# Last edge layer of a graph network: relation matrices as two fp16 parts instead of three bf16 parts, and 91 instead of 96 supertiles read from a table

## The chip, the cores and the metric

One Trainium2 chip, one core of it. The metric is the device time of one execution in microseconds (us), lower is better. A core has five engines with queues of their own: PE (TensorE, matrix products), DVE (VectorE), ACT (ScalarE), POOL (GpSimd) and SP (SyncE, which here only starts transfers). They meet through semaphores.

## What is computed

Four graph layers over 6250 nodes with 16 features and 206250 edges sorted by destination. The first runs on a dense adjacency matrix; the second gathers typed rows (8 edge types); the third is dense again; the fourth, which is changed here, is an edge layer with 90 relation types:

```
W_rel = matmul(w_comp, V).reshape(90, 16, 16)
h_src = h[src];  z_src = h_src @ Ws.T;  z_dst = h[dst] @ Ws.T;  z_e = he @ Ws.T
e   = concatenate([z_src, z_e, z_dst]) @ Wa.T
msg = einsum('ei,eio->eo', h_src, W_rel[rel_type]) * e
h_out = segment_sum(msg, dst)
x = x + h_out
```

## The kernel before

Edges are cut into tiles of 128, and eight tiles make a supertile of 1024 edges; there are 202 supertiles. In the last layer (`relation_layer`) each supertile is of one of three kinds, given by the line `PLAIN, LEAD, DIRECT = 11, 2, 96`.

- Plain, the first 11. POOL fetches the source rows h[src] by eight indirect transfers (L2191). Meanwhile PE builds a table in memory, for every node and every relation the finished product of row and matrix (`table_tile`, L2158, 49 tiles with three matmuls each; ACT and DVE evict them, SP stores them).
- Table, 96 of the other 191. POOL fetches the finished products by eight indirect transfers of 128 rows each (`fetch_table_rows`, L2205) into a ring of 12 row buffers. A buffer is free again when PE has summed the supertile that used it. DVE then only compares destinations (`make_dst`, L2230) and scales rows (`weigh_rows`, L2317, L2318).
- Matmul, the remaining 95. DVE writes one-hots of the source (`make_hot`, seven `tensor_scalar` at L2220 and L2221) and of the type (L2225, 90 partitions by 1024 edges). PE gathers the rows with 28 matmuls of 512 columns (`gather`, L2239), folds them with 16 small ones (`fold_rows`, L2254), and expands the type one-hots into one 16 by 16 matrix for each edge (`expand`, L2274).

The plain kind uses `expand` too, so `expand` runs for 106 supertiles. For each of the eight tiles of a supertile it makes three matmuls into the same half of a PSUM bank, one for each part of the relation matrices: `rel[:, 0..2, :]` holds a bf16 value, the bf16 remainder and the remainder of that. So there are 24 matmuls of 256 columns, with the type one-hots as the stationary operand (128 columns, 90 rows). DVE multiplies the result by the gathered rows and reduces it (`messages`, L2302 and L2294), and PE sums messages by destination (`add_up`, L2326).

The main loop runs over the supertiles that are not table ones, in rounds. In round i, PE's order is: fold and expand supertile i-1, gather supertile i, add up supertile i-2, and add up the table supertiles that lie behind i-2. DVE's order is: table rows behind i-2, one-hots of i+1, destinations and messages of i-1. A set of one-hots has two buffers, so DVE's `make_hot(i+1)` waits for PE's gather of i-1 (a semaphore). ACT takes the four gather banks out (L2245), then the folded rows (L2262), then the sums (L2337). POOL does nothing but fetch table rows. Which supertiles are table ones is spread evenly by integer division, about one between any two matmul ones.

The relation matrices are prepared much earlier, at the end of POOL's side work of the first layer (`split_relations`, L1614 to L1619): a load, a transposing copy, and four operations that make the three parts. The first layer has six dense passes (`one_pass`, 0 to 5) in which DVE scales a PSUM bank for each chunk of 448 nodes (L1420) and makes the next table.

Of the kernel before, what the change touches and what calls it, by code (L numbers as in the profile page):

```python
# [7 lines left out]
ALU = mybir.AluOpType  # L8
ACT = mybir.ActivationFunctionType
AX = mybir.AxisListType  # L10

P = 128
# [36 lines left out]
TOP = 14  # L49
# [17 lines left out]
LEAD1, DIRECT1, ROWS_AHEAD = 3, 80, 12  # L67
PLAIN, LEAD, DIRECT = 11, 2, 96
SPLIT_FROM = 4
# [52 lines left out]
def program(nc, t, wcols, out):  # L122
# [15 lines left out]
    def step(eng, ins):  # L138

        return done[eng].by(ins)  # L140

    def link(eng, ins):

        tok = step(eng, ins)
        need(eng, tok)
        return tok

    def sb(stack, name, shape, dt=F32):
        return stack.enter_context(nc.sbuf_tensor(name, list(shape), dt))
# [40 lines left out]
    var = sb(life, "var", [P, NT])  # L190
    rel = sb(life, "rel", [R90, 3, 256], BF16)
    t_u = sb(life, "t_u", [P, 3 * F])
    path = sb(life, "path", [P, 1], I32)
# [1086 lines left out]
    def layers_fast(h_tok):  # L1280
# [279 lines left out]
        def edge_terms(s):  # L1560
# [26 lines left out]
            make_rows(attr, s_attr[0], s_term[0])  # L1587
            split_relations(attr, s_attr[0])
            return [(x.sem, x.n) for x in s_term]

# [20 lines left out]
        def split_relations(attr, s_back):  # L1611

            relO, relT = (a[:, :, :].rearrange("p s c -> p (s c)")[0:R90, 0:256] for a in attr)
            need(pool, s_back.by(pool.dma_start(relO, rel_dram.rearrange("a r c -> (a r c)").rearrange("(r k) -> r k", k=256)), 16))  # L1614
            link(pool, pool.tensor_copy(relT.rearrange("r (o i) -> r o i", i=F), relO.rearrange("r (i o) -> r o i", o=F)))
            link(pool, pool.tensor_copy(rel[:, 0, :], relT))
            link(pool, pool.tensor_tensor(relO, relT, rel[:, 0, :], ALU.subtract))
            link(pool, pool.tensor_copy(rel[:, 1, :], relO))
            link(pool, pool.tensor_tensor(rel[:, 2, :], relO, rel[:, 1, :], ALU.subtract))  # L1619

# [5 lines left out]
        pool.wait_ge(s_used, NCH)  # L1626
        terms = edge_terms(side_work)
        st = one_pass(d, 1, st, [feature(d, "enc1", 128, 128, "enc_b1"), rows_table(d, 0, "enc2", 128, 64)], 64)
        for r in range(4):
# [5 lines left out]
            rows_table(d, 1, "dfc1_w", 32, 64, leaky=True, bias="dfc1_row")], 64)  # L1635
        st = one_pass(d, 3, st, [feature(d, "dec0", 128, 128, "dec_b0"), rows_table(d, 0, "dec1", 128, 64)], 64)
        st = one_pass(d, 4, st, [feature(d, "fold64", 128, 64, "dec_b1"), rows_table(d, 1, "dec2", 64, F)], F)
        d["spread"] = []
# [418 lines left out]
        def relation_layer(x_spread, terms, wx, w_ready):  # L2057
# [150 lines left out]
            def make_hot(i):  # L2208
# [14 lines left out]
                if i >= 3:  # L2223
                    dve.wait_ge(*w_tok[i - 3, SUP // 2 - 1])
                ty_tok[i] = c_ty.by(dve.tensor_scalar(tyh[i % 3][:, :], trow[b][:, :], iotaP[0:R90, :], None, ALU.is_equal))  # L2225

# [37 lines left out]
            def expand(i, between=()):  # L2264
                pe.wait_ge(*ty_tok[i])
                for q in range(SUP // 2):
                    if q == SUP // 4:
                        for m in between:
                            table_tile(m)
                    if i:  # L2270
                        pe.wait_ge(*prod_tok[i - 1, q])
                    for j in (2 * q, 2 * q + 1):
                        for p in range(3):
                            ins = pe.matmul(ps_w[q][:, (j % 2) * 256:(j % 2 + 1) * 256], tyh[i % 3][:, j * P:(j + 1) * P], rel[:, p, :], start=p == 0, stop=p == 2)  # L2274
                    if q % 2:
                        w_tok[i, q - 1] = w_tok[i, q] = c_w.by(ins)
# [260 lines left out]
```

## Time and profile before

| | us |
|---|---|
| median of 3 runs | 4388.06 |
| the three runs | 4388.06, 4360.72, 4389.13 |
| the profiled execution | 4367.42 |
| its span, first to last instruction | 4363.3 |
| PE busy / DVE busy in the span | 3616.4 (83%) / 2704.6 (62%) |
| ACT busy / POOL busy in the span | 1310.6 (30%) / 1907.4 (44%) |

### The profile page before, as it was taken

What the parts mean: (1) busy time and instruction counts of PE and PEld (TensorE: products, weight loads), DVE (VectorE), ACT (ScalarE), POOL (GpSimd) and SP (SyncE); (2) the same over time, 40 slices, a digit from 0 to 9 for tenths busy, and PEclk for the clock granted to TensorE, in tenths of its full rate; (3) what the DMA queues carried; (4) which work ended last, traced back from release to release, by engine and by line L of the source; (5) the groups of instructions that cost most, each with busy time, mean ns of one, the idle gap of its engine ahead of it and who ended that gap; (6) DMA issues with size and microseconds to landing.
All of it is one profiled execution on the core that took longest, in us unless ns stands there. A gap on an engine that the chain in (4) does not pass through costs nothing. (4 is left out here: it accounts for less than half of the span.)

```text
span 4363.3 us, 77744 instructions
## 1 busy us (share of the span) xinstructions
PE 3616.4 (83%) x28548; PEld 2114.8 (48%) x28548; DVE 2704.6 (62%) x6415; ACT 1310.6 (30%) x2874; POOL 1907.4 (44%) x1856
## 2 busy tenths in 40 slices
PE   6787879999998478888888886661899989998888
PEld 4566645544554234444444443330555555555555
DVE  8999953322212356767666674451777767777777
ACT  6999920011000123333233231330222212222222
POOL 1000006830000546777677640357366666666550
PEclk8999989999998689999899897765888888889998
DMA  5444467663366312222222227761222222222221
GB/s 148 83 82 82 66 267 297 218 235 121 151 246 259 88 41 51 51 51 51 47 51 51 51 45 249 271 206 13 41 44 44 44 39 44 44 44 44 39 43 40
DMA packets 471196, 445.62 MB, mean 102 GB/s; under 512 B 357554, under 2 KB 406610, under 8 KB 459676
## 3 DMA queue, kind: packets, MB, share of 16 engines
q1 hardware_dynamic: 389178, 391.82, 29.3%
q0 software_dynamic: 55216, 38.70, 6.4%
q10 hardware_dynamic: 26417, 10.05, 0.9%
q8 instruction: 232, 3.80, 0.4%
q14 instruction: 153, 1.25, 0.1%
HBM read 346.18 MB, written 95.85 MB: 101 GB/s over the span
## 5 line engine op out<-in xcount | busy, mean ns | idle before, releaser
L1814 POOL DMA_INDIRECT rows<-typed_table,ring x640 | 764.1, 1194 | 348.5 <-issue 182.0
L2239 PE MATMUL l_ps_g<-ring,h_part 128*128 128x512 f16 x2660 | 651.1, 405 | 108.4 <-issue 83.8
L1408 PE MATMUL L_ps<-ring,L_T 128*128 128x448 fp8e4 (+1 forms) x4606 | 671.2, 386 | 44.6 <-DMA ring<-adj 41.0
L2205 POOL DMA_INDIRECT ring<-typed_table,l_idxA x384 | 398.5, 1038 | 274.9 <-PE l_ps_x L2326 161.2
L1408 PEld LDWEIGHTS L_ps<-ring,L_T 128*128 128x128 f16 (+1 forms) x4606 | 327.8, 105 | 374.5 <-issue 62.0
L2205 POOL DMA_INDIRECT l_rows<-typed_table,l_idxA x384 | 392.1, 1021 | 252.6 <-PE l_ps_x L2326 146.6
L1875 DVE TENSOR_TENSOR dinvB<-G,tyh 128x1024 f16<-128x1024 f16 x244 | 288.4, 1223 | 337.5 <-ACT G L1862 215.3
L2239 PEld LDWEIGHTS l_ps_g<-ring,h_part 128*128 128x128 f16 x2660 | 275.5, 104 | 453.4 <-issue 190.7
L2245 ACT ACTIVATE l_sel<-l_ps_g 128x512 f16<-128x512 f32 x380 | 226.0, 597 | 855.5 <-PE l_ps_g L2239 375.5
L620 PE MATMUL cells<-keys,lows 128*128 128x147 f16 (+5 forms) x2744 | 372.7, 283 | 121.2 <-DVE keys L581 107.3
L2220 DVE TENSOR_SCALAR ring<-l_krow,W 128x1024 f16<-128x1024 f16 x570 | 234.7, 482 | 304.9 <-remote 178.0
L2274 PE MATMUL l_ps_w<-rel,l_tyh 90*128 90x256 bf16 x2544 | 383.3, 319 | 16.1 <-DVE ring L2302 10.8
L620 PEld LDWEIGHTS cells<-keys,lows 128*128 128x128 f16 x2744 | 286.4, 141 | 204.8 <-DVE keys L581 174.9
L581 DVE TENSOR_SCALAR keys<-build_or_wx,offset 128x441 f16<-128x441 f16 (+3 forms) x1438 | 366.5, 330 | 0.0
L1420 DVE SCALAR_TENSOR_TENSOR L_Y<-L_ps,L_scale,dinvB 128x448 f32<-128x448 f32 x84 | 57.4, 684 | 495.5 <-PE L_ps L1408 495.4
L1837 PE MATMUL ps_g<-ring_fifth,h_part 128*128 128x512 f16 x1464 | 353.4, 401 | 1.5 <-issue 1.4
L1837 PE MATMUL ps_g<-dinvB,h_part 128*128 128x512 f16 x1464 | 351.9, 399 | 1.0 <-issue 0.9
L698 ACT ACTIVATE ring<-cells 128x784 fp8e4<-128x784 f32 x392 | 324.2, 828 | 24.9 <-PE cells L620 24.6
L2274 PEld LDWEIGHTS l_ps_w<-rel,l_tyh 90*128 90x128 bf16 x2544 | 280.9, 113 | 88.6 <-issue 21.7
L1844 ACT ACTIVATE sel<-ps_g 128x512 f16<-128x512 f32 x488 | 263.2, 598 | 186.4 <-PE ps_g L1837 110.9
L2302 DVE TENSOR_TENSOR ring<-l_ps_w,l_G 128x512 f32<-128x512 f32 x380 | 258.4, 682 | 50.2 <-remote 46.5
L2294 DVE TENSOR_REDUCE l_msg<-ring 128x32 f32<-128x512 f32 x424 | 277.7, 676 | 0.0
(369 smaller groups left out, 4415.8 us busy)
## 6 DMA issues: line engine op xcount, KB each, us to landing
ring<-adj SPq DMA_DIRECT2D x67, 2744.0 KB, 10.9
adj<-ring SPq DMA_DIRECT2D x14, 2744.0 KB, 9.2
typed_table<-ring SPq DMA_DIRECT2D x49, 765.0 KB
ring_fifth<-src_div_mod_rows SPq DMA_DIRECT2D x122, 256.0 KB
l_krow<-src_div_mod_rows SPq DMA_DIRECT2D x95, 256.0 KB
l_trow<-type_row SPq DMA_DIRECT2D x106, 180.0 KB
attr<-in_he POOLq DMA_DIRECT2D x25, 512.0 KB, 6.5
klast<-last_keys SPq DMA_DIRECT2D x81, 128.0 KB
```

The source lines that it names most:

```text
L581: ins = dve.tensor_scalar(keys[g % OB][:, j, 0:C], iotaC[:, 0:C], offset[g // BG % 2][:, g % BG, j:j + 1], HIT, ALU.is_equal, ALU.mult)
L620: ins = pe.matmul(to, lows[g // QG % 3][:, :, g % QG * KT + j], made[:, (a1 - a) * NT:(b1 - a) * NT], start=j == FIRST[h], stop=j == LAST[ ...
L698: act.activation(ring[c % RING][:, :, gl * GD:(gl + 1) * GD].rearrange("p k (h d) -> p k h d", h=2), cells[g % CB][:, :, 0:HD * NT].rearra ...
L1408: ins = pe.matmul(bank[at:at + rows, 0:CH], d["T"][q][:, k, 0:rows], ring[r][:, k, :], start=n < side, stop=n >= NT - side, tile_position= ...
L1814: r_tok_[g] = r_in[b].by(pool.indirect_dma_start(rows[b][:, j, :], None, t1_dram, bass.IndirectOffsetOnAxis(ap=idxA[:, k * SUP + j:k * SUP ...
L1837: ins = pe.matmul(ps_g[2 * h + p][:, 0:HE], parts[p][:, j, :], hot[b][:, j, h * HE:(h + 1) * HE], start=False, stop=j == GJ - 2)
L1844: selt[i, h] = c_sel.by(act.activation(sel[b][2 * h + p][:, :], ps_g[2 * h + p][:, 0:HE], ACT.Relu))
L1875: typed_tok[i] = c_typed.by(dve.tensor_tensor(typed[b][:, p, :, :, :], gp, ty, ALU.mult))
L2205: rt_tok[g] = r_in[b].by(pool.indirect_dma_start(table_rows[b][:, j, 0:RC], None, t3_dram, bass.IndirectOffsetOnAxis(ap=idxA[:, k * SUP + ...
L2239: ins = pe.matmul(ps_g[p][:, 0:HE], parts[p][:, j, :], hot[b][:, j, h * HE:(h + 1) * HE], start=j == 0, stop=j == GJ - 1)
L2274: ins = pe.matmul(ps_w[q][:, (j % 2) * 256:(j % 2 + 1) * 256], tyh[i % 3][:, j * P:(j + 1) * P], rel[:, p, :], start=p == 0, stop=p == 2)
L2294: return c_msg.by(dve.tensor_reduce(m[:, 2 * q:2 * q + 2, 0:F], prod[q], AX.X, ALU.add))
```

## The change

Three things change.

1. The relation matrices are kept in two fp16 parts instead of three bf16 parts. `expand` makes 16 matmuls a supertile instead of 24.
2. fp16 has a narrow range, so each relation's matrix is multiplied by a power of two of its own before it is split, and the inverse power stands in the type one-hots: the `tensor_scalar` at L2225 writes not 1 but that power, with a second operation and a second scalar operand. POOL's four splitting operations go; in their place `scale_relations` runs seven DVE operations between passes 3 and 4 of the first layer, after a wait for POOL's transposing copy. The one-hots stay in a bf16 tile, so bf16 (stationary) meets fp16 (moving) in these matmuls.
3. `DIRECT` goes from 96 to 91: five supertiles move from the table kind to the matmul kind, so 100 matmul supertiles, 91 table ones and 11 plain ones.

```diff
-PLAIN, LEAD, DIRECT = 11, 2, 96
+PLAIN, LEAD, DIRECT = 11, 2, 91
     rel = sb(life, "rel", [R90, 3, 256], BF16)
+    rel_scale = sb(life, "rel_scale", [R90, 4])
...
-            link(pool, pool.tensor_copy(relT.rearrange("r (o i) -> r o i", i=F), relO.rearrange("r (i o) -> r o i", o=F)))
-            link(pool, pool.tensor_copy(rel[:, 0, :], relT))
-            link(pool, pool.tensor_tensor(relO, relT, rel[:, 0, :], ALU.subtract))
-            link(pool, pool.tensor_copy(rel[:, 1, :], relO))
-            link(pool, pool.tensor_tensor(rel[:, 2, :], relO, rel[:, 1, :], ALU.subtract))
+            return relT, step(pool, pool.tensor_copy(relT.rearrange("r (o i) -> r o i", i=F), relO.rearrange("r (i o) -> r o i", o=F)))
+
+        def scale_relations(relT, turned):
+
+            top, bits, up, down = (rel_scale[:, i:i + 1] for i in range(4))
+            hi, lo = (rel[:, p, :].bitcast(F16) for p in range(2))
+            need(dve, turned)
+            link(dve, dve.tensor_reduce(top, relT, AX.X, ALU.max, apply_absolute_value=True))
+            link(dve, dve.tensor_scalar(top, top, TINY, HUGE, ALU.max, ALU.min))
+            link(dve, dve.tensor_scalar(bits.bitcast(I32), top.bitcast(I32), 0x7F800000, None, ALU.bitwise_and))
+            link(dve, dve.tensor_scalar(up.bitcast(I32), bits.bitcast(I32), -1.0, float((254 + TOP) << 23), ALU.mult, ALU.add))
+            link(dve, dve.tensor_scalar(down, bits, 2.0 ** -TOP, None, ALU.mult))
+            link(dve, dve.tensor_scalar(hi, relT, up, None, ALU.mult))
+            link(dve, dve.scalar_tensor_tensor(lo, relT, up, hi, ALU.mult, ALU.subtract))
...
         st = one_pass(d, 3, st, [feature(d, "dec0", 128, 128, "dec_b0"), rows_table(d, 0, "dec1", 128, 64)], 64)
+        scale_relations(*relations)
         st = one_pass(d, 4, st, [feature(d, "fold64", 128, 64, "dec_b1"), rows_table(d, 1, "dec2", 64, F)], F)
...
-                ty_tok[i] = c_ty.by(dve.tensor_scalar(tyh[i % 3][:, :], trow[b][:, :], iotaP[0:R90, :], None, ALU.is_equal))
+                ty_tok[i] = c_ty.by(dve.tensor_scalar(tyh[i % 3][:, :], trow[b][:, :], iotaP[0:R90, :], rel_scale[:, 3:4], ALU.is_equal, ALU.mult))
...
-                        for p in range(3):
-                            ins = pe.matmul(ps_w[q][:, (j % 2) * 256:(j % 2 + 1) * 256], tyh[i % 3][:, j * P:(j + 1) * P], rel[:, p, :], start=p == 0, stop=p == 2)
+                        for p in range(2):
+                            ins = pe.matmul(ps_w[q][:, (j % 2) * 256:(j % 2 + 1) * 256], tyh[i % 3][:, j * P:(j + 1) * P], rel[:, p, :].bitcast(F16), start=p == 0, stop=p == 1)
```

## Rows read from the trace of the kernel before

**Rows 1.** The page's part 2: tenths in 40 slices of 109 us.

```profile
PEclk8999989999998689999899897765888888889998
```

**Rows 2.** Windows: length, PE, PEld, DVE, ACT, POOL busy (x), clock, DMA, GB/s.

```profile
2790.00:2850.00 60.00, 45.34 (x215) 25.08 (x214) 27.63 (x58) 28.16 (x57) 35.62 (x38) 0.68 0.83 301
2950.00:3060.00 110.00, 15.92 (x52) 5.99 (x51) 7.81 (x17) 2.07 (x4) 76.79 (x81) 0.52 0.12 11
3110.00:4244.00 1134.00, 1025.53 (x8128) 632.43 (x8127) 849.65 (x1948) 246.25 (x569) 687.66 (x665) 0.89 0.24 43
4244.00:4332.00 88.00, 87.46 (x799) 56.85 (x797) 80.41 (x184) 24.58 (x57) 0.00 (x0) 1.00 0.14 31
```

**Rows 3.** Timeline of PE, one round after POOL's last fetch: start, duration of the merged group.

```profile
4255.73 0.56 PE L2254 MATMUL l_ps_x<-fold,l_sel 128*128 128x16 f16 x16
4256.15 2.78 PE L2274 MATMUL l_ps_w<-rel,l_tyh 90*128 90x256 bf16 x24
4258.76 6.21 PE L2239 MATMUL l_ps_g<-ring,h_part 128*128 128x512 f16 x28
4264.90 0.94 PE L2326 MATMUL l_ps_x<-l_msg,ring 128*64 128x32 f32 x13
...
4266.68 0.56 PE L2254 MATMUL l_ps_x<-fold,l_sel 128*128 128x16 f16 x16
```

**Rows 4.** Timeline of PE, two rounds while POOL fetches.

```profile
3680.84 0.56 PE L2254 MATMUL l_ps_x<-fold,l_sel 128*128 128x16 f16 x16 [0.28 <-ACT l_sel L2245]
3681.25 4.30 PE L2274 MATMUL l_ps_w<-rel,l_tyh 90*128 90x256 bf16 x24
3685.35 8.09 PE L2239 MATMUL l_ps_g<-ring,h_part 128*128 128x512 f16 x28
...
3695.14 0.56 PE L2254 MATMUL l_ps_x<-fold,l_sel 128*128 128x16 f16 x16
...
3707.94 0.56 PE L2254 MATMUL l_ps_x<-fold,l_sel 128*128 128x16 f16 x16 [0.33 <-ACT l_sel L2245]
```

**Rows 5.** Timeline of ACT in the second of these rounds; in brackets the idle time before.

```profile
3704.42 0.60 ACT L2245 ACTIVATE l_sel<-l_ps_g 128x512 f16<-128x512 f32 x1 [2.43 <-PE l_ps_g L2239]
3707.28 0.60 ACT L2245 ACTIVATE l_sel<-l_ps_g 128x512 f16<-128x512 f32 x1 [2.27 <-remote]
```

**Rows 6.** Timeline of POOL in the same round: first and last of eight, and the next.

```profile
3695.48 1.43 POOL L2205 DMA_INDIRECT l_rows<-typed_table,l_idxA  x1 [4.12 <-PE l_ps_x L2326]
...
3704.80 0.95 POOL L2205 DMA_INDIRECT l_rows<-typed_table,l_idxA  x1 [0.31 <-issue]
...
3707.88 1.27 POOL L2205 DMA_INDIRECT l_rows<-typed_table,l_idxA  x1 [2.13 <-PE l_ps_x L2326]
```

**Rows 7.** Windows of single lines, in order L2254, L2205, L1854, L1854, L1814: length, busy (count).

```profile
3060.70:4332.40 1271.70, 55.76 (x1489) 45.22 (x1490) 0.90 0.23 42
...
3060.70:4332.40 1271.70, 696.47 (x672) 0.90 0.23 42
...
1560.40:2614.50 1054.10, 72.55 (x1856) 57.78 (x1856) 0.92 0.24 50
2577.70:2614.50 36.80, 2.79 (x80) 2.33 (x80) 1.00 0.18 46
...
1560.40:2614.50 1054.10, 699.15 (x576) 0.92 0.24 50
```

**Rows 8.** Groups of DVE instructions from 4255.7 to 4332.4: busy, mean ns, idle before.

```profile
L2220 DVE TENSOR_SCALAR ring<-l_krow,W 128x1024 f16<-128x1024 f16 x34 | 14.0, 482 | 1.7 <-PE l_ps_g L2239 1.6
```

**Rows 9.** Groups of DVE and PE over the span, by shape or from the page.

```profile
L581 DVE TENSOR_SCALAR keys<-build_or_wx,offset 128x392 f16<-128x392 f16 x392 | 125.9, 321 | 0.0
L388 DVE TENSOR_SCALAR dinvB<-dinvB 128x392 f16<-128x392 f16 x51 | 13.7, 320 | 0.1
L1408 PE MATMUL L_ps<-ring,L_T 128*128 128x448 fp8e4 (+1 forms) x4606 | 671.2, 386 | 44.6 <-DMA ring<-adj 41.0
```

**Rows 10.** Timeline of DVE at the start of pass 4 of the first layer.

```profile
1195.33 0.68 DVE L1420 SCALAR_TENSOR_TENSOR L_Y<-L_ps,L_scale,dinvB 128x448 f32<-128x448 f32 x1 [4.58 <-PE L_ps L1408]
```

More of the change, by code:

```diff
@@ L1587, in edge_terms @@
             make_rows(attr, s_attr[0], s_term[0])
-            split_relations(attr, s_attr[0])
-            return [(x.sem, x.n) for x in s_term]
+            return [(x.sem, x.n) for x in s_term], split_relations(attr, s_attr[0])
         def make_rows(attr, s_part_in, s_rows):
@@ L1626, in layers_fast @@
         pool.wait_ge(s_used, NCH)
-        terms = edge_terms(side_work)
+        terms, relations = edge_terms(side_work)
         st = one_pass(d, 1, st, [feature(d, "enc1", 128, 128, "enc_b1"), rows_table(d, 0, "enc2", 128, 64)], 64)
```

## The prediction

> **What bounds the kernel now.** I read the page first: its clock line shows the whole second half of the span below full clock, except near the end [rows 1]. Then windows of the last layer. The plain stage is full of transfers (301 GB/s) and of PE work at a low clock. Then come 110 us in which PE is busy for 15.9 and POOL fills the row ring with its first 96 fetches. Then 1134 us of rounds with POOL fetching, and at last 88 us in which POOL is done, the clock is full and PE has no gap [rows 2].
>
> The timeline of that last stretch gives the price of an undisturbed round: 0.42 us fold, 2.61 expand, 6.14 gather, 1.78 sums, in all 10.95 us from fold to fold [rows 3]. PE sets it, but DVE is close: over seven rounds the one-hots waited 1.7 us in total, so DVE needs about 10.7 us of each 10.95 [rows 8]. A round at this price is the exception. From 3060.7 to 4332.4 us there are 1489 folding matmuls, 16 to a round, so 93 rounds in 1271.7 us, 13.67 us each [rows 7]. The difference is read in two neighbouring rounds. In one of 12.80 us (3695.14 to 3707.94) PE had issued its gather on time, but ACT found the third bank at 3704.42 and the fourth at 3707.28, 2.86 us apart where an undisturbed quarter of the gather takes 1.5 [rows 4, 5]. At that time POOL is in a run of eight fetches, from 3695.48 to 3705.75; the banks come free as the run ends, and POOL then waits for PE [rows 6]. In the other round, 14.30 us, expand and gather take 4.10 and 8.09 us for 2.61 and 6.21: the clock is at 1.2 GHz for part of it, after the long, thin stretch at the end of the late round. What the two lose together, 5.2 us, comes once in two rounds, that is once in 16 fetches.
>
> Is the loss one of rounds or of fetches? Over the whole stage: 1271.7 - 93 x 10.95 + 1.5 (two rounds without table sums) is 254.9 us, and 672 fetches are 42 sixteens: 6.07 us for each (more than 5.2, since a few delays are longer). The typed layer has the same pattern with shorter rounds: 116 rounds in 1054.1 us with 576 fetches, and five rounds without fetches in 36.8 us, 7.36 each. So 1054.1 - 116 x 7.36 = 200 us over 36 sixteens, 5.6 us for each [rows 7]. Two layers whose rounds differ by half pay nearly the same for 16 fetches. I take it as a price of fetches, not of rounds.
>
> **The change, part by part.**
>
> *Eight matmuls fewer in a round.* 2.61 us for 24 is 0.109 each at full clock [rows 3], so a round loses 0.87 us: PE 10.08. Without a table supertile behind it, PE also loses one of two sums, 0.73 of the 1.78, and needs 9.35. DVE keeps its 10.7 us, and without table work (destinations, two small scalings, about 1.0) 9.7. So in an undisturbed round DVE becomes the bound, and the gain is 0.25 instead of 0.87. In disturbed ones PE stays the bound: two of them would take 27.1 - 1.74 = 25.4 us, and DVE needs 21.4. No row shows bf16 one-hots against fp16 matrices. The nearest is the dense pass, which mixes an fp16 stationary operand with an 8-bit moving one: 386 ns from start to end for 448 columns, a mean over both clocks, in which no surcharge stands out [rows 9]. I take none; a pair of types that streamed at two thirds of the rate would eat the whole saving, which is rival 4.
>
> *A second operation in the type one-hots.* A `tensor_scalar` with compare and multiply took 321 ns for 392 fp16 columns, one with the compare alone 320 [rows 9]. The second operand there is a constant and here a pointer, so nothing to 0.1 us; if the instruction fell to half its rate, 0.3 to 0.5 us of DVE in a round, hidden in disturbed rounds, 5 to 10 us in all.
>
> *Five supertiles from table to matmul.* POOL makes 40 fetches fewer: 632 after the ring is full, 39.5 sixteens. PE and DVE get five more rounds: 98 for 93. ACT's and SP's added work lies beside them: ACT is busy 246 of 1134 us and the transfers 0.24 [rows 2].
>
> *Preparation.* POOL drops four small operations long before its next work. DVE gets seven, on 256 columns or one; by the nearest row (0.68 us for 448 columns) about 2 us with their waits, at a place where DVE idles for 4.58 us until PE ends a chunk [rows 10]. POOL's copy, which the first of them waits for, lies two passes earlier. Nothing, at most 2 us if it were late.
>
> *The plain stage.* Eleven expansions lose 8 matmuls each, at half clock 0.21 us each: 19 us of PE. The stage also moves 301 GB/s of table, and PE is busy 45 of 60 us [rows 2]. So between 0 and 19 us; I take 5, near the lower end, since the first table fetch waits for the last table store.
>
> *The 110 us of first fetches* stay: 96 fetches with the ring of 12 unchanged, and PE has little to do in them.
>
> *Sum* for the 98 rounds: 79 table supertiles are fetched meanwhile, with PE rounds of 10.08 (796 us) and 39.5 sixteens at 6.07 (240 us); 12 more are in the ring at the end, at DVE's 10.7 (128 us); seven or so rounds have no table supertile, at 9.7 (68 us). Together 1232 us for 1271.7: 40 us less. With 5 from the plain stage, 45 us less than the profiled execution's 4367.4, so 4322. That execution lies 21 us below the median of the runs shown, whose other two are at 4361 and 4389; the forecast against the median is 4388 - 45 = 4343.
>
> **A rule that speaks against it.** After the thin stretch of 12.80 - 9.17 = 3.6 us at the end of the late round (sums, waits, then a fold), the clock falls; after the 1.78 us of an undisturbed round it never does [rows 3, 4]. The change makes dense work shorter and lets DVE bind. The Trainium skill, "TensorE: Matmul & The Clock Gate", section "A second HAM failure mode: psum-queue depth-cycling", says that small idle gaps between groups of matmuls can make the clock swing and cost throughput. The rows agree for long gaps; by it the change could cost time, priced as rival 3.
>
> Another page points away from my reading of the late banks. POOL's fetches do wait for DVE's fp16 one-hots (1.43 against 0.95 us), while PE's results are late beside POOL's run [rows 5, 6]. The Trainium skill, "SBUF — State Buffer", section "Who interferes with whom", has the first and denies the second: PE and ACT never wait on anyone. By it the loss would not be one of fetches but of rounds, and 98 for 93 rounds at 2.74 lost each would make the sum about 30 us worse. I go by the rows.
>
> **Rivals.**
>
> 1. *The late round gives nothing back.* Its end is tied to POOL: the fourth bank came 1.5 us after POOL's run ended [rows 5, 6]. If PE's banks are released by that, PE reaches them 0.87 us earlier and waits 0.87 us longer. Price: 39.5 x 0.87 = 34 us, so 4388 - 11 = 4377. For it: the two times. Against it: only the last two of four banks were late, and the typed layer pays no more for the same fetches although its rounds are shorter.
>
> 2. *The delay shrinks.* If it hits whatever PE has under way late in POOL's run, the gather ends 0.87 us earlier and more of it escapes; a late round loses less than 1.87 us, its thin stretch is shorter, and the clock falls less often. A half of the 39.5 losses of 5.2 us gone is 100 us more: about 4243. Nothing in the rows favours it beyond that all four banks of the other round were on time.
>
> 3. *The clock falls in every round.* This is the one on the slower side. Where DVE binds, PE waits at the sums: the thin stretch grows from 2.2 us (sums and fold) to 2.8. It decides if a stretch of this length is enough for 1.2 GHz: then a round costs 3.4 us more (10.08 + 3.4 = 13.5, as the 14.30 us round cost 3.35). 98 rounds at 13.5, with the late banks' 39.5 x 1.87, are 1397 us: 125 us more than now, and with the plain stage's 5 the end is 4508. If only the 19 undisturbed rounds pay it (2.8 each over DVE's 10.7), 53 us go, and the end is 4396. Against it: at 2.2 us the clock stays at 1.00 over 88 us [rows 2].
>
> 4. *It doesn't do what it says*: the mixed types or the two-operand one-hots run at a lower rate. Then PE needs 10.95 us as now: 91 rounds at 10.95, 7 at 10.22 and 240 us for the fetches are 1308 us, 36 more than now, and the end is 4424.
>
> **How the numbers follow.** Forecast 0.47, rival 1 0.22, rival 2 0.11, rival 3 0.13 (mostly its small form), rival 4 0.04, nothing of these 0.03. The likeliest stands: 4343 us. Its own range is 4320 to 4370, from the unknown costs (plain stage 14, operations 10) and from a before that spreads over 28 us. The whole range takes in rival 1 and the small form of rival 3 and goes part of the way to rival 2: 4290 to 4402. One per cent, 44 us, is about what a measurement of this kernel can tell from no change. The forecast lies on that line; a little over half of it and rival 2 give faster by over 1% 0.38; rival 3's large form, half of rival 4 and the upper tail of rival 3's small form give slower 0.11; the rest is 0.51.
>
> **What would show it.** Right: 16 expansions in about 1.75 us at full clock; fold to fold 10.7 us in the last stretch with DVE's one-hots hardly waiting; two rounds with POOL in about 25.4 us; 39 or 40 late rounds; the clock at 0.88 to 0.90 from 3110 us on. Rival 1 shows as late rounds still of 12.8 us and others of 13.5. Rival 3 shows as a clock below 1.00 after POOL's last fetch, which is what would make me most wrong. A change in the first three layers of more than some 10 us would not be this change's doing, but would stand in the time.

## The result: 1.4% slower, and the profile after

| | before | after |
|---|---|---|
| median | 4374.39 us (4 runs) | 4420.65 us (4 runs) |
| the runs | 4388.06, 4360.72, 4389.13, 4341.10 | 4415.76, 4437.60, 4425.54, 4391.42 |
| profiled execution / its span | 4367.42 / 4363.3 | 4415.76 / 4411.8 |

The ratio is 1.0136, with a 95% interval from 1.0092 to 1.0179. Forecast were 45 us less; measured are 46 more. The two traces keep together to the last table matmul (2917.5 us before, 2922.2 after). The second round of folds starts 28.7 us later (3060.8 against 3089.5), the last 50.7 us later (4332.4 against 4383.1). So some 24 us were lost beside the first 96 fetches and 22 in the rounds. Inside the 4.7 us ahead of them, the unchanged typed layer took 10 us longer (last chunk of pass 5 at 1422.5 before and 1419.5 after, last gather at 2620.3 and 2627.6), and from there to the last table matmul the changed kernel is 2.6 us shorter (297.2 against 294.6), where the forecast took 5.

The clock line of the page after stands beside [rows 1]:

```profile
PEclk8999989999998689998899987765998889989989
```

Windows of the changed kernel (columns as in [rows 2]): the first fetches, the rounds with POOL, the rounds after its last fetch.

```profile
2930.00:3090.00 160.00, 33.15 (x153) 14.26 (x154) 31.26 (x69) 5.63 (x12) 96.90 (x101) 0.53 0.14 24
3090.00:4302.00 1212.00, 1038.11 (x8119) 609.95 (x8115) 939.07 (x2136) 269.49 (x620) 662.39 (x632) 0.90 0.22 44
4302.00:4383.00 81.00, 81.00 (x746) 51.24 (x744) 79.72 (x183) 24.45 (x57) 0.00 (x0) 1.00 0.13 34
```

The clock did not fall (0.90 beside POOL's fetches, 1.00 behind them). The window of the folding line, which answers to the first of [rows 7]:

```profile
3089.40:4383.20 1293.80, 67.90 (x1572) 52.84 (x1573) 0.91 0.22 43
```

98 rounds in 1293.8 us. An undisturbed one, on PE's timeline, for [rows 3]:

```profile
4312.57 0.56 PE L2264 MATMUL l_ps_x<-fold,l_sel 128*128 128x16 f16 x16
4312.98 1.91 PE L2284 MATMUL l_ps_w<-rel,l_tyh 90*128 90x256 f16 x16
4314.73 6.21 PE L2249 MATMUL l_ps_g<-ring,h_part 128*128 128x512 f16 x28
4320.87 0.94 PE L2336 MATMUL l_ps_x<-l_msg,ring 128*64 128x32 f32 x13
...
4322.65 0.56 PE L2264 MATMUL l_ps_x<-fold,l_sel 128*128 128x16 f16 x16
```

It lasts 10.08 us: the expansions take 1.75 instead of 2.61, as forecast, with no surcharge for mixed types. Now a pair of rounds while POOL fetches, which answers to [rows 4]:

```profile
3974.92 0.56 PE L2264 MATMUL l_ps_x<-fold,l_sel 128*128 128x16 f16 x16
3975.34 1.91 PE L2284 MATMUL l_ps_w<-rel,l_tyh 90*128 90x256 f16 x16
3977.08 6.21 PE L2249 MATMUL l_ps_g<-ring,h_part 128*128 128x512 f16 x28
...
3985.00 0.23 PE L2264 MATMUL l_ps_x<-fold,l_sel 128*128 128x16 f16 x3
3985.68 0.17 PE L2264 MATMUL l_ps_x<-fold,l_sel 128*128 128x16 f16 x1 [0.45 <-issue]
3986.39 0.17 PE L2264 MATMUL l_ps_x<-fold,l_sel 128*128 128x16 f16 x1 [0.54 <-issue]
3987.10 0.43 PE L2264 MATMUL l_ps_x<-fold,l_sel 128*128 128x16 f16 x11 [0.53 <-issue]
3987.38 2.50 PE L2284 MATMUL l_ps_w<-rel,l_tyh 90*128 90x256 f16 x16
3989.67 4.32 PE L2249 MATMUL l_ps_g<-ring,h_part 128*128 128x512 f16 x14
3995.66 1.67 PE L2249 MATMUL l_ps_g<-ring,h_part 128*128 128x512 f16 x7 [1.67 <-issue]
3999.84 1.68 PE L2249 MATMUL l_ps_g<-ring,h_part 128*128 128x512 f16 x7 [2.51 <-ACT l_sel L2255]
...
4003.23 0.56 PE L2264 MATMUL l_ps_x<-fold,l_sel 128*128 128x16 f16 x16
```

The first round is free of any delay, 10.08 us. The second takes 18.23: PE's matmuls come singly, 0.7 us apart, for 2.1 us, and two of four gather banks are late. Together 28.3 us; before, such a pair took 27.1. POOL's timeline in the same stretch, for [rows 6]:

```profile
3975.26 1.49 POOL L2215 DMA_INDIRECT l_rows<-typed_table,l_idxA  x1 [6.26 <-PE l_ps_x L2336]
...
3984.79 1.24 POOL L2215 DMA_INDIRECT l_rows<-typed_table,l_idxA  x1 [0.30 <-issue]
3987.60 0.98 POOL L2215 DMA_INDIRECT l_rows<-typed_table,l_idxA  x1 [1.57 <-remote]
...
3996.40 0.95 POOL L2215 DMA_INDIRECT l_rows<-typed_table,l_idxA  x1 [0.30 <-issue]
4003.57 1.50 POOL L2215 DMA_INDIRECT ring<-typed_table,l_idxA  x1 [6.23 <-PE l_ps_x L2336]
```

POOL's eight fetches take 10.8 us (3975.26 to 3986.03), the new round 10.08. So the next buffer is already free when the run ends; POOL goes on after 1.57 us with eight more, and PE is delayed from the end of the first run until 2.5 us after the end of the second. Before, runs of eight were parted by pauses of 2.1 and 4.1 us [rows 6]. The pair shown stands for many: of the last 87 rounds, 39 take about 10 us and 29 from 18 to 21.

**The size of it.** The loss for 16 fetches, by the prediction's own formula, is the rounds' total less undisturbed rounds: 1293.8 - (98 x 10.08 - 7 x 0.73) = 311.1 us over 39.5 sixteens, 7.9 us each, where before had 6.07. Each such loss comes from one profiled execution.

### The profile page after: what moved, and what is told of

Read it like the earlier page. It is cut to its first block and busy times, and to the rows that moved or that the text cites. A ratio compares the mean times of both kernels' runs of the same rounds, so it can differ in the third digit from the quotient of the medians.

```text
span 4411.8 us, 76811 instructions
## 1 busy us (share of the span) xinstructions
PE 3550.7 (80%) x28000; PEld 2041.3 (46%) x28000; DVE 2760.0 (63%) x6512; ACT 1320.7 (30%) x2899; POOL 1876.4 (43%) x1812
## 3 DMA queue, kind: packets, MB, share of 16 engines
q0 software_dynamic: 53936, 38.35, 5.6%
## 5 line engine op out<-in xcount | busy, mean ns | idle before, releaser
L2249 PE MATMUL l_ps_g<-ring,h_part 128*128 128x512 f16 x2800 | 700.4, 407 | 209.3 <-issue 139.3
L2249 PEld LDWEIGHTS l_ps_g<-ring,h_part 128*128 128x128 f16 x2800 | 287.5, 104 | 588.0 <-issue 250.4
L2215 POOL DMA_INDIRECT l_rows<-typed_table,l_idxA x344 | 353.6, 1028 | 238.0 <-PE l_ps_x L2336 114.6
L2255 ACT ACTIVATE l_sel<-l_ps_g 128x512 f16<-128x512 f32 x400 | 236.0, 597 | 729.3 <-PE l_ps_g L2249 395.9
L2230 DVE TENSOR_SCALAR ring<-l_krow,W 128x1024 f16<-128x1024 f16 x600 | 247.5, 481 | 218.2 <-PE l_ps_g L2249 210.4
L1854 ACT ACTIVATE sel<-ps_g 128x512 f16<-128x512 f32 x488 | 263.1, 598 | 154.9 <-PE ps_g L1847 90.6
L2284 PE MATMUL l_ps_w<-rel,l_tyh 90*128 90x256 f16 x1776 | 274.7, 317 | 40.7 <-issue 28.8
L2304 DVE TENSOR_REDUCE l_msg<-ring 128x32 f32<-128x512 f32 x444 | 290.4, 674 | 0.0
L2312 DVE TENSOR_TENSOR ring<-l_ps_w,l_G 128x512 f32<-128x512 f32 x400 | 271.2, 680 | 0.6 <-PE l_ps_w L2284 0.4
L1847 PEld LDWEIGHTS ps_g<-ring_fifth,h_part 128*128 128x128 f16 x1464 | 143.9, 102 | 204.6 <-issue 61.3
```

The source lines that it names most:

```text
L1847: ins = pe.matmul(ps_g[2 * h + p][:, 0:HE], parts[p][:, j, :], hot[b][:, j, h * HE:(h + 1) * HE], start=False, stop=j == GJ - 2)
L2215: rt_tok[g] = r_in[b].by(pool.indirect_dma_start(table_rows[b][:, j, 0:RC], None, t3_dram, bass.IndirectOffsetOnAxis(ap=idxA[:, k * SUP + ...
L2249: ins = pe.matmul(ps_g[p][:, 0:HE], parts[p][:, j, :], hot[b][:, j, h * HE:(h + 1) * HE], start=j == 0, stop=j == GJ - 1)
L2304: return c_msg.by(dve.tensor_reduce(m[:, 2 * q:2 * q + 2, 0:F], prod[q], AX.X, ALU.add))
L2312: prod_tok[i, q] = c_prod.by(dve.tensor_tensor(prod[q], wq, gq, ALU.mult))
```

## The experiments

The same comparison was made for each kernel against the kernel before on its own chip. The chips differ: the kernel before had medians of 4374, 4464, 4371, 4462 and 4445 us beside the kernels told of here, and of 3828 on one chip, of which more below. Totals of rounds are windows of the folding line, as above. They start at the second round of folds and say what one execution did.

### Two halves of the change: e1_parts_only, e2_direct_only

```diff
 e1 (changed kernel):      -PLAIN, LEAD, DIRECT = 11, 2, 91   +PLAIN, LEAD, DIRECT = 11, 2, 96
 e2 (kernel before):       -PLAIN, LEAD, DIRECT = 11, 2, 96   +PLAIN, LEAD, DIRECT = 11, 2, 91
```

> The changed kernel with DIRECT back at 96: only the two parts (and what goes with them) are left. 93 rounds and 42 sixteens of fetches after the ring is full. Theory 1: the shorter round makes each delay of PE beside POOL longer, 8.2 us for 16 fetches instead of 6.1, whatever DIRECT is. Then the rounds take 93 x 10.08 + 42 x 8.2 = 1282 us against 1271.7 before, and with the 20 us that the first fetches took longer the ratio to before is about 1.007. Theory 2: the longer delays come from the other placement of the 91 table supertiles; with 96 the price stays 6.1, the rounds take 93 x 10.08 + 42 x 6.1 = 1194 us, and the kernel is 75 us faster, ratio about 0.983.

> The kernel before with DIRECT = 91 and three bf16 parts as they were. 98 rounds of 10.95 us undisturbed, 39.5 sixteens. Theory 1 (the price of 16 fetches depends on the length of the round, not on DIRECT): 98 x 10.95 + 39.5 x 6.1 = 1314 us for 1271.7, ratio 1.010. Theory 2 (the placement of 91 raises the price to 8.2): 98 x 10.95 + 39.5 x 8.2 = 1397 us, ratio 1.029.

Measured: e1 1.0088 (1.0045 to 1.0130), e2 1.0055 (1.0019 to 1.0091). Both halves cost, and their sum is the whole 1.4%. The two parts alone, which take 0.87 us of PE's work out of every round, make the kernel slower: 93 rounds in 1323.2 us, a loss of (1323.2 - 935.9) / 42.5 = 9.1 us for 16 fetches. The first of these rounds still lies in the 96 first fetches; without it the loss is 8.7. e2 has 98 rounds in 1322.2 us, (1322.2 - 1068.0) / 39.5 = 6.4 each, nearly the price of before. The unchanged typed layer took nearly the same in both traces (1248.8 and 1252.2 us from first to last gather), so the two compare well. The longer delays come with the two parts and not with the placement of 91.

### The third matmul put back: e5_third_again

```diff
+            link(dve, dve.memset(rel[:, 2, :].bitcast(F16), 0.0))
-                        for p in range(2):
+                        for p in range(3):
```

> Two parts, power-of-two one-hots and DIRECT = 96 as in the parts-only run, but a third matmul over a part of zeros is put back, so expand takes 2.6 us again and everything else of the change stays. Theory 1 (the shorter round of PE is what lengthens the delays): the pairs of rounds are as before, 12.8 to 13 and 14.3 us, and the ratio to before is 1.00 (0.997 to 1.003). Theory 4 (types, one-hots or preparation cost the time): the ratio stays at the 1.009 of the parts-only run.

Measured: 1.0025 (0.9993 to 1.0056), within the range of the first theory. Types, two-operand one-hots and preparation are all still in; only PE's 0.87 us are back. 93 rounds took 1307.9 us, a loss of 6.75 us for 16 fetches, or 6.1 without the first round, of which a part lies in the first fetches. That is the price of before, and it points to PE's shorter round as what made e1 slower.

It is not proof. e1 ran on another chip, its interval touches this one, and e7 and e8 below, which are nearly the changed kernel on e5's chip, measured 1.0010 and 1.0081 there. The execution profiled is the fastest of e5's twelve (4332.56 us against a median of 4377.67), and its unchanged typed layer took 1158.4 us where e8's took 1204.8. So the loss of this one execution may be low for a reason that has nothing to do with the edit.

### Other transfers in place of the indirect ones: e3, e3b, e6

These three leave out the row numbers of the table supertiles: consecutive rows of the table are transferred instead of the rows that the edges name, so the layer's result is not computed.

```diff
 e3 (changed), e3b (before)
-                for j in range(SUP):
-                    rt_tok[g] = r_in[b].by(pool.indirect_dma_start(...
+                rt_tok[g] = r_in[b].by(pool.dma_start(table_rows[b][:, :, 0:RC], t3_dram[g * 1024:(g + 1) * 1024, :].rearrange("(p e) c -> p e c", e=SUP)), 16)
 e6 (changed): in the loop over j
+                    rt_tok[g] = r_in[b].by(pool.dma_start(table_rows[b][:, j, 0:RC], t3_dram[(g * SUP + j) * P:(g * SUP + j + 1) * P, :]), 16)
```

> The changed kernel, in which each table supertile gets its 1024 rows in one plain transfer of consecutive rows by POOL instead of eight indirect transfers: the same bytes, other rows. If the delays of PE are made by the indirect transfers, none is left: rounds of 10.08 us, 98 of them in about 990 us, and the 125 us of first fetches shrink to some 30, so about 4410 - 300 - 95 = 4015 us. If they are made by the traffic or by the semaphores between PE and POOL, rounds of 18 to 20 us stay.

> The same edit of the kernel before: one plain transfer for eight indirect ones. If the indirect transfers make the delays: 93 rounds of 10.95 us, 1018 us, and the first fetches short, so about 4363 - 250 - 80 = 4030 us. The two-part kernel with 91 is then faster than this one by some 15 to 30 us (98 x 10.08 = 988 against 93 x 10.95 = 1018). If the two differ as the real kernels do (+1.4%), the fetches are not what turned the saving into a loss.

> The changed kernel with eight plain transfers of 128 rows by POOL for each table supertile, in place of the eight indirect ones: as many transfers and as many semaphore updates, other rows. If the number of POOL's transfers or of their semaphore updates delays PE, the rounds are as in the changed kernel (28 us for two). If it is the indirect form, there is no delay: 10.5 us each, as with one plain transfer.

Measured, one execution each: e3 4099.06, e3b 4054.58, e6 4014.09 us. The 45 us between e3 and e3b are not in the changed stage: the last gather of the typed layer starts at 2707.7 us in one and 2657.4 in the other, and no line of that layer differs. So one execution of the same code differs by 50 us from another in that layer, on one chip. The rounds, first of e3:

```profile
3043.90:4065.40 1021.50, 54.82 (x1574) 45.72 (x1575) 1.00 0.24 55
```

then of e3b:

```profile
3001.30:4019.70 1018.40, 51.98 (x1491) 43.36 (x1492) 1.00 0.24 53
```

No delay is left in either, at full clock throughout. And the change is worth nothing: 98 rounds in 1021.5 us against 93 in 1018.4. e3's rounds take 10.51 us and not 10.08, and a row of PE's groups over eight of them (3406.8 to 3490.9) says why:

```profile
L2282 PE MATMUL l_ps_w<-rel,l_tyh 90*128 90x256 f16 x128 | 16.6, 273 | 2.1 <-DVE ring L2310 2.1
```

The expansions wait for the PSUM banks that DVE empties: DVE binds, at 10.51 us. e6 moves as many packets and bytes through POOL's queue as the changed kernel (53936 packets, 38.35 MB in both), and has no delay either (98 rounds in 1021.4 us). But its run of eight is shorter too, 4.21 us:

```profile
3405.99 4.21 POOL L2215 DMA_DIRECT2D ring<-typed_table  x8 [6.30 <-PE l_ps_x L2335]
```

So the amount of traffic and the number of semaphore updates are ruled out. That the indirect form itself delays PE, rather than the length of POOL's run or the scattered rows, isn't shown.

### Is it the count of fetches? e8_shift_four

In the changed kernel most delays of 0.7 us steps start where the count of all indirect fetches since the start reaches a multiple of 16. e8 has four fetches more in the plain stage, into columns that nobody reads.

```diff
+                for j in range(4 if r == PLAIN - 1 else 0):
+                    r_in[RT - RG + b].by(pool.indirect_dma_start(
+                        rows[b][:, j, F:2 * F], None, h_dram, ...srcA[:, r * SUP + j:r * SUP + j + 1]...), 16)
```

> The changed kernel with four more indirect fetches in the plain stage, into columns that nobody reads, so that the count of all fetches passes a multiple of 16 in the middle of a supertile's eight and no longer at its end. In the changed kernel PE's stumbles (matmuls 0.7 us apart) start within 1 us of every sixteenth fetch. If the count rules, they now start after the fourth fetch of a run of eight. If the end of POOL's run or its wait for PE rules, they stay at the end of a run. The time: unknown, within 1% of the changed kernel (ratio 1.005 to 1.022).

Measured: 1.0081 (1.0043 to 1.0118). The 1088th fetch is now the one at 3592.11 us, in the middle of a run that ends with that of 3597.10. The loss for 16 fetches is 8.1 us (98 rounds in 1301.0 us). PE:

```profile
3597.94 0.17 PE L2267 MATMUL l_ps_x<-fold,l_sel 128*128 128x16 f16 x1 [0.38 <-issue]
3598.65 0.17 PE L2267 MATMUL l_ps_x<-fold,l_sel 128*128 128x16 f16 x1 [0.54 <-issue]
```

POOL:

```profile
3597.10 1.24 POOL L2218 DMA_INDIRECT l_rows<-typed_table,l_idxA  x1 [0.30 <-issue]
3599.85 1.03 POOL L2218 DMA_INDIRECT l_rows<-typed_table,l_idxA  x1 [1.51 <-remote]
```

The steps stay at the end of POOL's run, 5.8 us after the count's multiple. The count falls. A delay once in 16 fetches is the rhythm of two rounds and not a property of the fetches, and with it falls the ground on which the prediction carried its price over to a shorter round.

### Breaking or shifting POOL's runs: e7, e9 to e12

e7 was meant to stop POOL after four of eight fetches, until the first half of the gather in the round behind the one whose buffer is filled again. e9 to e12 make the fetch of a supertile behind round i wait for PE's gather of round i - 3, its end (h = 1: e9, e10, e11) or its first half (h = 0: e12); POOL then leads by three rounds and the 96 fetches in a row ahead of the rounds (the burst) are gone.

```diff
 e7 (changed)
+                    if j == SUP // 2 and g >= RT:
+                        r = next(x for x in range(n) if g - RT in after[x])
+                        if (r + 1, 0) in gat:
+                            pool.wait_ge(*gat[r + 1, 0])
 e9 (changed), e10 (before), e11 (changed, DIRECT 96): h = 1; e12 (changed): h = 0
+                if (i - 3, h) in gat:
+                    pool.wait_ge(*gat[i - 3, h])
```

> The changed kernel, in which POOL makes four of the eight fetches of a supertile when the buffer is free and then waits for the first half of PE's gather in the next round before the other four. Theory 1 in the form that dense runs of fetches cost more than spread ones: runs of 16 with one pause of 1.6 us give way to runs of 8 or fewer, the price of 16 fetches falls from 8.2 to about 6, and 39 sixteens give 80 us back: ratio to before about 0.995. Rival: the price belongs to the number of fetches alone (each sixteenth one is followed by a delay, as the trace of the changed kernel shows at counts 1152, 1168, 1184 ...); then nothing changes against the changed kernel, ratio 1.014.

> The changed kernel, in which POOL's fetch of a table supertile that belongs behind round i also waits for the end of PE's gather in round i - 3. So POOL leads PE by some three rounds, and the 96 fetches in a row ahead of the first rounds (125 us in which PE issues a matmul every 0.7 to 2.8 us) are gone: two or three supertiles stand in their place, 30 us. The other nine supertiles, 4.5 sixteens, are fetched beside rounds at 8.2 us each: 37 us back. Expected: 95 - 37 = about 58 us less than the changed kernel, ratio to before about 1.001. If the lead is too short, DVE waits for rows in most rounds and the kernel is slower than the changed one (ratio over 1.014).

> The same wait in the kernel before (three parts, DIRECT = 96): 95 us of the burst less, 4.5 sixteens more beside rounds at 6.1 us, 27 us: 68 us less, ratio to before about 0.984. With e9 it tells what the change is worth under paced fetches: theory 1 (the two-part round is dear wherever POOL follows its rhythm) has this one ahead by 1 to 2%; if the phase of POOL's runs against PE's round is what counts, and not the round's length, the two are equal or the changed one is ahead.

> The wait of e9 with two parts and DIRECT back at 96. From the runs with 96 and 91 alone, 96 was 0.5% better for both; so about 0.5% below e9, ratio about 0.996.

> As e9, but POOL waits for the first half of the gather in round i - 3 and not for its end, so a run of eight starts 3.1 us earlier in PE's round. If the phase of the run against PE's round decides how much PE loses, this differs from e9 by 1% or more to either side; if only the number and density of fetches count, the two agree within 0.4%.

| | kernel | ratio to before | interval |
|---|---|---|---|
| e7 | changed, halves | 1.0010 | 0.9975 to 1.0046 |
| e9 | changed, gather's end | 1.0464 | 1.0411 to 1.0517 |
| e10 | before, gather's end | 1.0718 | 1.0671 to 1.0765 |
| e11 | changed with 96, gather's end | 1.0691 | 1.0646 to 1.0736 |
| e12 | changed, gather's middle | 0.9870 | 0.9831 to 0.9908 |

e7's wait never held POOL: that half of the gather was long done, and in each of the 79 runs behind the first twelve the fifth fetch starts 0.3 us after the fourth ends, as all others do. First, fourth and fifth fetch of a run:

```profile
3999.28 1.50 POOL L2219 DMA_INDIRECT ring<-typed_table,l_idxA  x1 [7.58 <-PE l_ps_x L2340]
...
4003.83 0.95 POOL L2219 DMA_INDIRECT ring<-typed_table,l_idxA  x1 [0.30 <-issue]
4005.08 0.94 POOL L2219 DMA_INDIRECT ring<-typed_table,l_idxA  x1 [0.31 <-issue]
```

So e7 is in effect the changed kernel once more, and says nothing on broken runs. What it does say is how far such kernels lie apart: 1.0010 for it and 1.0081 for e8 on one chip, 1.0136 for the changed kernel on another. Its loss for 16 fetches, over 97 rounds behind the first fetches (1264.6 us), is 7.4 us.

e9 to e11 missed: the burst is gone and the kernels are 5 to 7% slower. In e9, PE in a round of 19.3 us:

```profile
3845.08 3.40 PE L2251 MATMUL l_ps_g<-ring,h_part 128*128 128x512 f16 x14
3854.54 5.89 PE L2251 MATMUL l_ps_g<-ring,h_part 128*128 128x512 f16 x14 [6.07 <-ACT l_sel L2257]
```

and POOL, first and last of eight:

```profile
3841.86 1.15 POOL L2217 DMA_INDIRECT l_rows<-typed_table,l_idxA  x1 [7.82 <-PE l_ps_g L2251]
...
3851.26 0.95 POOL L2217 DMA_INDIRECT l_rows<-typed_table,l_idxA  x1 [0.30 <-issue]
```

Such a run of eight holds PE up for 8 to 9 us, until 2.3 us after it ends, although a pause of 7.82 us stood ahead of it; 50 of the last 87 rounds take 18 or 19 us. DVE waits for no table rows from 3200 us on, so it isn't that POOL's lead is too short. ACT's timeline shows what the second half of the gather waited for:

```profile
3853.80 1.09 ACT L2257 ACTIVATE l_sel<-l_ps_g 128x512 f16<-128x512 f32 x2 [5.61 <-remote]
```

PE's first half ended at 3848.5; ACT took its two banks out 5.3 us later, 1.6 us after POOL's run. In the changed kernel a run that starts 1.3 us later in PE's round passes without any. e12's wait lets a run start 3.1 us earlier than e9's, mid gather, and the kernel is 6% faster than e9 on the same chip. Its phase isn't a fixed one: by e12's trace 50 of POOL's runs waited for the gather, and most of the others followed the run ahead of them. Its start, for the first window above:

```profile
2956.00:3080.00 124.00, 97.93 (x675) 53.59 (x673) 92.54 (x208) 24.36 (x52) 73.96 (x67) 0.82 0.29 66
```

PE is busy for 98 of 124 us after the last table matmul (in the changed kernel 33 of 160). That is where e12 gains. Its rounds are dearer than those of the changed kernel (98 in 1380.2 us, 8.9 us lost for 16 fetches), but from POOL's first table fetch to the last round of folds it takes 1397 us (from 2982.9), the changed kernel 1448 (from 2935.4). e12 is the one version that beats both kernels; on the chip without delays it was not run, and e15, which is near it, gains nothing there.

### A chip without the delays: e13 to e16

```diff
 e13: e12's wait in the kernel before     e14: e12 with DIRECT = 96     e16: the changed kernel as it is
 e15 (changed)
+                if (i - 3, SUP // 2 - 1) in w_tok:
+                    pool.wait_ge(*w_tok[i - 3, SUP // 2 - 1])
```

> The wait of e12 (first half of the gather of round i - 3) in the kernel before, three parts and DIRECT = 96. Phase theory: PE's loss is set by where POOL's run of eight lies in PE's round; the run starts mid gather in both kernels, so the loss per supertile is the same and each round is 0.87 us longer. 93 rounds at 14.08 + 0.87 us are 1390 us against e12's 1380: ratio to before 0.989, and two parts win back only what 91 instead of 96 costs. Round-length theory (a two-part round is dearer wherever POOL follows PE): this one is 20 us or more below e12, ratio 0.982 or less.

> The same wait with two parts and DIRECT = 96. With the loss per supertile unchanged, five rounds of 10.08 us fewer and five supertiles of fetches (about 4 us of loss and 0.7 of sums each) more: 25 us below e12, ratio to before 0.981. If POOL, at nearly one run of eight for each round, becomes too dense, the loss per supertile grows as in e11 against e9 and the ratio is above 0.99.

> The changed kernel, POOL waiting for the end of PE's expansions in round i - 2: its run starts 3.1 us earlier in PE's round than in e12 (2.2 us after the round's start) and ends 2 us into the next round. Phase theory: no other start is known to be as good as mid gather, so between e12 (0.987) and the changed kernel's own phase (0.3 us after the round's start, 1.014): 0.990 to 1.005. If only the missing burst made e12 fast, this one is as fast, 0.985 to 0.989.

> The changed kernel once more, beside the others on their chip: ratio to before 1.009 to 1.018 as measured at first, so that e12 to e15 can be set against it without a change of chip.

This batch ran on a chip on which the kernel before takes 3828.03 us. Measured: e13 1.0009 (0.9991 to 1.0026), e14 1.0162 (1.0134 to 1.0191), e15 1.0074 (1.0047 to 1.0101), e16 1.0028 (1.0011 to 1.0046). None of the phase questions could be answered there, since POOL's runs delay nothing. A window of e16 in the rounds:

```profile
3110.00:3330.00 220.00, 213.96 (x1915) 130.83 (x1914) 217.87 (x501) 63.59 (x146) 175.19 (x148) 1.00 0.31 56
```

PE's expansions and POOL's fetches over seven rounds of it (3248.4 to 3322.4), groups by shape:

```profile
L2284 PE MATMUL l_ps_w<-rel,l_tyh 90*128 90x256 f16 x112 | 14.6, 273 | 2.1 <-DVE ring L2312 2.1
```

```profile
L2215 POOL DMA_INDIRECT l_rows<-typed_table,l_idxA x35 | 42.0, 1201 | 10.7 <-issue 10.7
```

POOL fetches without a pause, indirectly, and PE waits for DVE alone. Rounds of 10.54 us, DVE-bound: 98 took 1045.6 us against e13's 93 of 10.95 in 1018.4. Not all of e16's rounds are so: DVE waits 19.3 us in all for the rows of 16 supertiles, and in a few rounds the clock falls. One of 14.06 us, with gather matmuls at 1.2 GHz in it, is this window:

```profile
3353.90:3368.00 14.10, 13.14 (x78) 6.29 (x76) 14.03 (x30) 2.86 (x6) 10.77 (x11) 0.76 0.38 78
```

This is the change by itself, without the delays of the other chips: 0.3% slower. In e14, with 96 at this pace, POOL is too slow: DVE waits 93 us in all for the rows of 64 supertiles.

### Two and three parts with the same wait: e17, e18

e17 is e12's kernel and e18 is e13's, for a chip with the delays.

> The kernel of e12 once more (changed kernel, POOL waits for the first half of the gather of round i - 3). On a chip that delays PE beside POOL's fetches (before near 4370 to 4460 us): 0.987 again, 0.983 to 0.991. On one that doesn't (before near 3830 us): POOL needs 10.3 us for eight fetches and rounds take 10.5, so nothing is gained over the changed kernel, 1.000 to 1.008.

> The kernel of e13 once more (three parts, DIRECT = 96, same wait), for a chip that delays PE. Phase theory: the loss per supertile is as in e17 and only PE's 0.87 us a round and the five rounds differ, so within 0.5% of e17, 0.984 to 0.993. Round-length theory: 20 us or more below e17, 0.982 or less. On a chip without the delays: 1.001 as before.

The kernel before took 4445.22 us there. Measured: e17 0.9931 (0.9894 to 0.9968), e18 1.0130 (1.0076 to 1.0183). Both theories missed. (One of e17's eleven executions took 6731.16 us and is not in its ratio.) With this wait the two-part kernel is 2% faster than the three-part one: 98 rounds in 1350.1 us against 93 in 1481.3, or by the formula 8.2 and 9.9 us lost for 16 fetches. The wait is the same but not the phase: POOL stood at it 48 times in e17 and 82 times in e18. Where POOL follows the ring's own rhythm, three parts were better: behind the first fetches 6.1 (before), 6.4 (e2) and 6.1 (e5) against 7.9 (changed), 8.1 (e8), 7.4 (e7) and 8.7 (e1). So a shorter round isn't dearer by itself; it was in that rhythm.

## Why the prediction was wrong

*What was right.* Eight matmuls at 0.109 us: the undisturbed PE round is 10.08, its expansions 1.75 us. No surcharge for bf16 against fp16. The preparation costs nothing (pass 4 starts at 1195.0 us, before at 1195.3). The clock holds in the changed kernel, and rival 3 did not come; in e16, where DVE binds, the clock fell in a few rounds and held in most. DVE would bind at about 10.7: e3 and e16 show 10.51 and 10.54. The rounds of 10.08 at the end of the changed kernel do not speak against this, since PE's delays gave DVE a lead; in e16 a round of 14.06 us is followed by six of 10.07 or 10.08 and one of 10.33 before 10.53 is back. The second operation in the one-hots takes 0.06 us (0.528 against 0.468), within the 0.1 allowed:

```profile
L2235 DVE TENSOR_SCALAR l_tyh<-l_trow,iotaP,rel_scale x111: 527/528/543, 2777.1 to 4366.7; 90x1024 bf16<-90x1024 f16 x111
```

*The step that failed* is "I take it as a price of fetches, not of rounds". The price of 16 fetches was put at 6.07 us and carried to a round that is 0.87 us shorter; it is 7.9 there (8.7 with 96). Over 39.5 sixteens that is 311 us for 240, 71 more. The undelayed rounds were 9 us cheaper than in the sum (982.7 for 992, since DVE did not bind), so 1232 became 1293.8, and the 40 us gained became 22 lost. The agreement with the typed layer (5.6 us) was one of two numbers that happen to lie near each other: that layer, unchanged, took from 1158.4 to 1231.3 us in four executions on one chip (e5 to e8), up to 1.8 us for 16 fetches apart. So one trace can't fix such a price. That it is higher in the shorter round rests on the seven traces above, and best on the two pairs whose typed layers agree to 10 us: before and changed (6.1, 7.9), e2 and e1 (6.4, 8.7). e8 shows that no count of fetches is behind it, e5's trace has the old price with PE's 0.87 us put back, e9 and e12 show that the same fetches cost 14.8 us for 16 ((1646.5 - 982.7) / 45) or 8.9 ((1380.2 - 982.7) / 44.8) according to where POOL's run starts in PE's round. Rival 1 had the right direction against the forecast and a part of the mechanism (the end of the delay is tied to the end of POOL's run, 1.5 to 2.5 us after it); it was held to giving nothing back, and the delay gave back more than was saved.

*The second step* is that the 110 us of first fetches stay. They took some 24 us longer in the profiled execution. Before, PE got through its first gather in the first 20 us of POOL's burst; POOL's first table fetch and PE's gather:

```profile
2928.25 1.01 POOL L2205 DMA_INDIRECT ring<-typed_table,l_idxA  x1 [2.63 <-DMA typed_table<-ring]
...
2938.45 7.78 PE L2239 MATMUL l_ps_g<-ring,h_part 128*128 128x512 f16 x28
```

In the changed kernel the burst starts at 2935.4 and this gather ends behind it; its last half:

```profile
3060.86 2.98 PE L2249 MATMUL l_ps_g<-ring,h_part 128*128 128x512 f16 x7 [68.77 <-issue]
3071.97 3.17 PE L2249 MATMUL l_ps_g<-ring,h_part 128*128 128x512 f16 x7 [8.13 <-ACT l_sel L2255]
```

From POOL's first table fetch to the first fold it is 19 us before and 141 after, but 18 in e1, 19 in e5, 18 in e7 and 15 in e8, which is the changed kernel with four fetches more. So the late gather isn't the change's own.

*What the change is worth.* Even with no delay the 40 us weren't there. Five supertiles moved are five rounds more, and e3's 98 rounds in 1021.5 us stand against e3b's 93 in 1018.4. The prediction's 40 us rested on PE-bound rounds of 10.08 for 79 of 98, which hold only while delays keep DVE ahead. The 5 us of the plain stage came as 2.6 in the one pair of traces, too little to tell from nothing.

*What stays open.* Which part of the chip holds PE up beside POOL's indirect runs, and why one chip of those used shows nothing of it. In e9 ACT starts late on banks that PE had long filled, so it may be the signals between the engines as well as PE itself. The Trainium skill, "SBUF — State Buffer", section "Who interferes with whom", says that PE and ACT never wait on anyone. In e16 this is so: in the stretch shown PE waits for DVE only. On the other chips matmuls with all inputs ready come 0.7 us apart at the end of POOL's runs, so the rows there contradict it. Why a run that starts at one place of PE's round passes free and 1.3 us earlier does not is open too; that the place of POOL's wait decides is shown (e9 against e12), the rule is not. And the size of the change's own cost is open: kernels that are the changed one or nearly so measured 1.0136, 1.0081, 1.0010 and, without the delays, 1.0028.

## What to carry to other kernels

A stall of one engine beside another's bursts has no price of its own: it depends on where the bursts fall in the round, and a change of the round's length moves them. Before a saving is put against such a stall, compare the length of the round with that of the burst: here 10.95 us left a pause behind eight fetches of 10.3 to 10.8 us, and 10.08 left none. (A pause alone isn't enough: e9 had one of 7.8 us.) A wait of one line that takes the burst away was worth more than the change (e12: 0.987 and, on another chip, 0.993 of the kernel before), but the same line is dear at another place (1.046), and for the three-part kernel (1.013): measure it with the kernel that it is for, and on more than one chip. And look in the trace whether a wait that was put in is ever waited for: e7's wasn't.

## What the hardware showed that was not expected

- The same kernel takes 4374 us on one chip and 3828 on another, and the difference lies in the two layers with indirect fetches (the typed layer's last gather starts at 2620.3 us before, at 2445.3 in e16, while the last chunk of pass 5 stands at 1422.5 and 1415.3).
- While POOL makes 96 indirect fetches in a row, PE is busy for 33 of 160 us. The first half of its gather comes in single matmuls 2.1 or 2.8 us apart, with nothing that the profile shows them waiting for; then there is none from 2991.5 to 3060.9 us, and ACT takes out the first bank only at 3060.1.
- On the chip without delays POOL itself is slower where DVE is busier: 728 fetches in 1077.6 us (1.48 each) in e16, 768 in 1056.7 (1.38 each) in e13, although e13's also wait for the gather. Of e16's last 632, the 256 that start beside a one-hot instruction of DVE took 1.52 us in the mean, the other 376 took 0.95.
- The typed layer, which is the same in all kernels and makes 640 indirect fetches, took from 1158.4 to 1231.3 us in single executions on one chip, so one profile says little about a difference of some 50 us beside such fetches.
